# Flamingo-style two-layer block with a top-2 mixture of experts: expert results added to their rows in DRAM instead of on VectorE

## The reference, cut to what matters

```python
def _L1_ffn_ref(x, W_gate, b_gate, W_e, b_e):
    TOP_K = 2
    logits = x @ W_gate + b_gate
    _, top_idx = jax.lax.top_k(logits, TOP_K)
    y_all = jax.nn.relu(jnp.einsum('bsd,edh->bseh', x, W_e) + b_e)
    y = jnp.take_along_axis(y_all, top_idx[..., None], axis=2)
    return y.mean(axis=2)
...
x = x + jnp.tanh(g_ffn[1]) * _L1_ffn_ref(_layernorm(x, axis=-1), ...)
```

## Time and profile before

| | before |
|---|---|
| median of 3 runs | 1082.39 us |
| the profiled execution's own time | 1082.77 us |
| its span (first to last instruction) | 1080.9 us |
| TensorE busy | 959.7 us (89%) |
| VectorE busy | 619.8 us (57%) |
| ScalarE busy | 337.3 us (31%) |
| GpSimd busy | 424.6 us (39%) |
| mean granted TensorE clock | 0.942 of full speed |

### The profile page before, as it was taken

The page is one execution under the profiler, slowest core; times in us unless marked ns, Lnnn a source line. Parts: engine busy times, 40 slices in busy tenths (PEclk is TensorE's granted clock), DMA queues, the critical chain, the costliest instruction groups (busy, mean ns, idle before and its releaser), DMA issues.

```text
span 1080.9 us, 14248 instructions
## 1 busy us (share of the span) xinstructions
PE 959.7 (89%) x4851; PEld 737.6 (68%) x4851; DVE 619.8 (57%) x1067; ACT 337.3 (31%) x599; POOL 424.6 (39%) x414
## 2 busy tenths in 40 slices
PE   4899999999998999999999979979999998629991
PEld 4677778877777777778777658637777674227770
DVE  5864764465752665653647655645655555873334
ACT  4322142132241141331221311225444556312320
POOL 3541522421620522422415243464333424764540
PEclk9899999999999999999999998979999995659996
DMA  8020110010200110200200211060000003213447
GB/s 288 10 79 1 68 40 10 36 43 30 78 1 12 40 39 30 78 1 10 78 1 1 70 44 54 17 226 21 11 10 10 0 1 114 92 56 124 147 127 262
DMA packets 37592, 63.77 MB, mean 59 GB/s; under 512 B 5601, under 2 KB 13217, under 8 KB 37409
## 3 DMA queue, kind: packets, MB, share of 16 engines
q1 hardware_dynamic: 32416, 50.70, 13.7%
q0 software_dynamic: 3680, 12.06, 3.4%
q10 hardware_dynamic: 1440, 0.24, 0.1%
HBM read 52.77 MB, written 10.22 MB: 58 GB/s over the span
## 4 chain that ended last, share of the span: by engine, by line
PE 81%; DVE 8%; issue 4%; DMA 2%; ACT 2%; POOL 2%; ACTq 1%; SPq 0%; POOLq 0%; DVEq 0%
PE ps L1289 17%; PE ps L1290 16%; PE ps L1291 16%; PE ps L1501 5%; PE ps L1378 5%; PE ps L1520 5%; PE ps L1386 4%; PE ps L1508 3%; PE ps L1394 2%; PE ps L1488 2%; DVE at_lo L969 1%; DMA rows_in<-h_rows,gather_i 1%; DVE stats L844 1%; PE ps L1528 1%; POOL k_blk L543 1%
## 5 line engine op out<-in xcount | busy, mean ns | idle before, releaser
L476 POOL TENSOR_TENSOR q_t<-rot_a,rot_b 128x512 f32<-128x512 f32 x64 | 82.3, 1287 | 145.8 <-DVE rot_b L894 145.8
L1289 PE MATMUL ps<-wo_hi,at_hi 128*128 128x512 f32 x256 | 108.7, 425 | 18.7 <-DVE at_lo L969 11.9
L892 DVE TENSOR_TENSOR rot_a<-ps,cos 128x512 f32<-128x512 f32 x80 | 55.3, 692 | 112.6 <-PE ps L1291 112.6
L543 POOL TENSOR_TENSOR k_blk<-k_raw,m_full 32x512 f32<-32x512 f32 x64 | 80.8, 1262 | 90.1 <-ACT k_raw L752 86.3
L1289 PE MATMUL ps<-xt_hi,wq_hi 128*128 128x512 f32 x256 | 108.1, 422 | 0.2 <-issue 0.2
L1291 PE MATMUL ps<-xt_hi,wq_lo 128*128 128x512 f32 x256 | 101.4, 396 | 0.0
L1290 PE MATMUL ps<-xt_lo,wq_hi 128*128 128x512 f32 x256 | 101.4, 396 | 0.0
L1291 PE MATMUL ps<-wo_hi,at_lo 128*128 128x512 f32 x256 | 100.2, 391 | 0.0
L1290 PE MATMUL ps<-wo_lo,at_hi 128*128 128x512 f32 x256 | 100.0, 391 | 0.0
L697 ACT ACTIVATE at_hi<-ps 128x512 fp32r<-128x512 f32 x64 | 38.2, 597 | 189.2 <-PE ps L1394 189.2
L974 DVE TENSOR_TENSOR X<-ps,X 128x512 f32<-128x512 f32 x64 | 44.3, 691 | 84.6 <-PE ps L1291 84.6
(11 more groups left out here) (219 smaller groups left out, 2206.3 us busy)
## 6 DMA issues: line engine op xcount, KB each, us to landing
wq_raw<-in_wq SPq DMA_DIRECT2D x8, 1024.0 KB, 5.6
wo_raw<-in_wo SPq DMA_DIRECT2D x8, 1024.0 KB, 5.3
w_raw<-in_we SPq DMA_DIRECT2D x8, 1024.0 KB, 9.6
y_in<-y_rows SPq DMA_DIRECT2D x16, 256.0 KB, 5.1
X<-in_x SPq DMA_DIRECT2D x4, 512.0 KB, 13.3
wk_raw<-in_wk SPq DMA_DIRECT2D x8, 256.0 KB, 2.8
q_t<-in_ctx_t SPq DMA_DIRECT2D x2, 1024.0 KB, 10.4
wv_raw<-in_wv SPq DMA_DIRECT2D x4, 512.0 KB, 4.5
```

Source lines behind the costliest of these rows:

```text
L476: nc.gpsimd.tensor_tensor(dst, rot_a[:, r % 2, :], rot_b[:, r % 2, :], ALU.add).then_inc(rope_ok, 1)
L543: last = nc.gpsimd.tensor_tensor(k_blk[part, j, grp, :, hd, :], heads(k_raw[part, grp, :]), heads(m_full[part, j, :]), ALU.mult)
L892: nc.vector.tensor_tensor(heads(rot_a[:, r % 2, :]), heads(bank), bcast(cos[:, :], 4), ALU.mult)
L1289: nc.tensor.matmul(dst, w_hi, x_hi, start=start and k == 0, stop=False)
```

## The change

A DRAM tensor `sum_rows` (1024 rows and 128 spare ones) takes the place of `y_rows`. It is filled from `X` before the loop. Each scatter adds its rows to `sum_rows` in the DMA (`compute_op=ALU.add`). Both choices of a row now go to the same DRAM row n, so each scatter waits for the scatter before it to have landed. The factor tanh of the gate is applied by a second ScalarE instruction per tile. The loads into `y_in` and the 16 VectorE additions at the end are gone, and the output is copied from `sum_rows`, DRAM to DRAM. Padding rows of all tiles share the 128 spare rows.

```diff
-        y_rows = nc.dram_tensor("y_rows", (TOP * N + NC * P, D), F32).ap()
+        sum_rows = nc.dram_tensor("sum_rows", (N + P, D), F32).ap()
...
 # SyncE, behind the load of be_b
-            yv = y_rows[0:TOP * N].rearrange("(k b p) d -> p b k d", k=TOP, b=B)
+            for b in range(B):
+                sp.wait_ge(x3_ok, CREDIT + b + 1)
+                sp.dma_start(sum_rows[b * P:(b + 1) * P, :], X[:, b, :]).then_inc(sum_in, 16)
+            sp.dma_start(sum_rows[N:N + P, :], X[:, 0, :]).then_inc(sum_in, 16)
+
             for j in range(3):
                 sp.wait_ge(y_out[j], 16 * ((NT - j + 2) // 3))
-            for q in range(KT):
-                for b in range(2 * q, 2 * q + 2):
-                    for k in range(TOP):
-                        sp.dma_start(y_in[:, b, k, :], yv[:, b, k, :]).then_inc(y_ok[q], 16)
             for b in range(B):
-                sp.wait_ge(x4_ok, CREDIT + b + 1)
-                sp.dma_start(out[b], X[:, b, :]).then_inc(out_done, 16)
+                sp.dma_start(out[b], sum_rows[b * P:(b + 1) * P, :]).then_inc(out_done, 16)
             sp.wait_ge(out_done, 16 * B)
...
 # GpSimd
             def put_rows(i):
                 gp.wait_ge(r_ok, CREDIT + i + 1)
-                nc.gpsimd.indirect_dma_start(y_rows[:, :], bass.IndirectOffsetOnAxis(scatter_i[:, i:i + 1], 0),
-                                             r_d[:, i % 3, :], None).then_inc(y_out[i % 3], 16)
+                if i >= 1:
+                    gp.wait_ge(y_out[(i - 1) % 3], 16 * ((i - 1) // 3) + 16)
+                nc.gpsimd.indirect_dma_start(sum_rows[:, :], bass.IndirectOffsetOnAxis(scatter_i[:, i:i + 1], 0),
+                                             r_d[:, i % 3, :], None, compute_op=ALU.add).then_inc(y_out[i % 3], 16)
...
             gp.wait_ge(si_ok, CREDIT + 1)
+            gp.wait_ge(sum_in, 16 * (B + 1))
             for i in range(NT):
...
 # ScalarE
-                nc.scalar.activation(r_d[:, i % 3, :], ps[:, 4 + i % 4, :], ACT.Relu, scale=1.0 / TOP).then_inc(r_ok, 1)
+                nc.scalar.activation(r_d[:, i % 3, :], ps[:, 4 + i % 4, :], ACT.Relu, scale=1.0 / TOP).then_inc(relu_ok, 1)
+                ac.wait_ge(relu_ok, CREDIT + i + 1)
+                nc.scalar.activation(r_d[:, i % 3, :], r_d[:, i % 3, :], ACT.Copy, scale=tanh_g[:, 3:4]).then_inc(r_ok, 1)
...
 # VectorE
-            nc.vector.tensor_tensor(scatter_i[:, :], padding[:, :], listed[:, :], ALU.add).then_inc(si_ok, 1)
+            nc.vector.tensor_tensor(scatter_i[:, :], padding[:, :], row_of[:, :], ALU.add).then_inc(si_ok, 1)
...
-            for b in range(B):
-                ve.wait_ge(y_ok[b // 2], 64)
-                nc.vector.scalar_tensor_tensor(X[:, b, :], y_in[:, b, 0, :], tanh_g[:, 3:4], X[:, b, :], ALU.mult, ALU.add).then_inc(y0_ok, 1)
-                ve.wait_ge(y0_ok, CREDIT + b + 1)
-                nc.vector.scalar_tensor_tensor(X[:, b, :], y_in[:, b, 1, :], tanh_g[:, 3:4], X[:, b, :], ALU.mult, ALU.add).then_inc(x4_ok, 1)
```

More of the change, by code:

```diff
@@ L190, in flamingo_gated_two_layers @@
         place[0] = at_1
-        y_in = over("y_in", [P, B, TOP, D])
         w_lo = sb("w_lo", [P, EX, KT, D], F32R)
@@ L298, in flamingo_gated_two_layers @@
         of_ok, gi_ok, si_ok = sem("of_ok"), sem("gi_ok"), sem("si_ok")
-        rows_ok, y_out, y_ok = ([sem(f"rows_ok{j}") for j in range(3)], [sem(f"y_out{j}") for j in range(3)],
-                                [sem(f"y_ok{j}") for j in range(KT)])
-        tr_mm, gh_ok, glo_ok, y0_ok = sem("tr_mm"), sem("gh_ok"), sem("glo_ok"), sem("y0_ok")
+        rows_ok, y_out, sum_in, relu_ok = ([sem(f"rows_ok{j}") for j in range(3)], [sem(f"y_out{j}") for j in range(3)], sem("sum_in"),
+                                           sem("relu_ok"))
+        tr_mm, gh_ok, glo_ok = sem("tr_mm"), sem("gh_ok"), sem("glo_ok")
         weh_ok, wel_ok, gate_mm, gt_ok, gt_mm, sel_ok, rank_ok = (sem("weh_ok"), sem("wel_ok"), sem("gate_mm"), sem("gt_ok"), sem("gt_mm"),
                                                            sem("sel_ok"), sem("rank_ok"))
-        y2_mm, td_ok, r_ok, x4_ok, out_done = sem("y2_mm"), sem("td_ok"), sem("r_ok"), sem("x4_ok"), sem("out_done")
+        y2_mm, td_ok, r_ok, out_done = sem("y2_mm"), sem("td_ok"), sem("r_ok"), sem("out_done")
         N_SMALL, N_LATE = 10, 12
@@ L612, in _ @@
             start_counts(ac, (ot_ev, prep_a, gates_ok, hth_ok, cth_ok, wkh_ok, wvh_ok, wqh_ok, wo_hi_ok, v_ok, th_ok, ex_ok, ah_ok, wbh_ok,
-                              lge_ok, zt_ok, pq_ev, p_ok, pt_ok, gelu_ok, weh_ok, r_ok, gt_ok, gh_ok))
+                              lge_ok, zt_ok, pq_ev, p_ok, pt_ok, gelu_ok, weh_ok, relu_ok, r_ok, gt_ok, gh_ok))
             def hi_part(dst, raw, done):
@@ L838, in _ @@
                               x1_ok, bbg_ok, lg_ok, lgm_ok, lgs_ok, lgi_ok, al2_ok, zw_ok, tb_ok, hc_ok, mm_ok, mf_ok,
-                              cv_ok, mx_ok, sb_ok, oi_ok, on_ok, tc_ok, x3_ok, sel_ok, rank_ok, td_ok, x4_ok, wel_v, tri_ok,
-                              slot_ok, hot_ok, of_ok, gi_ok, si_ok, glo_ok, y0_ok))
+                              cv_ok, mx_ok, sb_ok, oi_ok, on_ok, tc_ok, x3_ok, sel_ok, rank_ok, td_ok, wel_v, tri_ok,
+                              slot_ok, hot_ok, of_ok, gi_ok, si_ok, glo_ok))
             def row_stats(n, b, j, ready, before=0):
@@ L1660, in _constants @@
         np.triu(np.ones((P, P)), 1), np.broadcast_to(np.arange(P) - P, (P, P)), np.broadcast_to(P * np.arange(NC + 1), (P, NC + 1)),
-        tok.reshape(P, B * TOP), TOP * N + 1 + np.arange(P)[:, None] + P * np.arange(NC)[None, :],
+        tok.reshape(P, B * TOP), np.broadcast_to(N + 1 + np.arange(P)[:, None], (P, NC)),
         np.broadcast_to(np.arange(NC), (P, NC))], axis=1).astype(np.float32)
```

## The result

The changed kernel takes 1120.04 us (median of 4 runs, 1118.47 to 1121.44) against 1082.32 of the kernel before (one run more than in the median above): a ratio of 1.034, 95% interval 1.0315 to 1.0365, so 3.4% slower. The profiled execution took 1120.19 us with a span of 1118.3. The forecast was 1105 with a range of 1082 to 1145: the right side and inside the range, 15 us too low.

A forecast was written before the change was run, and what follows sets the result against it. The prediction took TensorE and POOL's scatter-gather chain to hold the loop before, and single-file scatters after; 994.9 + 23 L with L = 4.8 gave 1105.3 us (loop +29.9, end -7.4), range 1082 to 1145.

The forecast's parts named there:

- The bound of the loop: Expert loop after the change: scatters run one behind another and set the period, 4.9 us against 3.57 before; chance 68%.
- L: Time of one adding scatter on POOL, from start of issue to landing: taken as 4.8 us, between 3.99 and 5.74.
- The step from landing to the next issue: On POOL between one scatter's landing and the next scatter's issue: taken as 0.1 us, once in each of 22 periods.
- The first scatter: Start of the loop's scatters on POOL: issue at 980.59, which is 979.98 plus 0.61 us for the second ScalarE instruction.
- The end: From the last scatter's issue on: 15.1 us instead of 22.5, a gain of 7.4, with 10 us for the DRAM copies.
- The filling of `sum_rows`: SyncE's 9 stores before the loop: landed by some 958, 22 us before the first scatter waits for them, at no cost.
- The gather's chain of the kernel before: Loop before: gathers queued behind scatters on POOL, 11.0 us per three tiles; the second ScalarE instruction makes it 11.6.
- The wait costs nothing: Rival for the loop: L below 3.77, period 3.87 by the gather's chain, about 1079 us, not slower; chance 15%.
- The dear issue: Rival on POOL: issuing an adding scatter could double or treble the 0.97 us; L = 8 gives 1179 us; chance 9%.
- The clock fell: Rival for TensorE in the loop: low clock level throughout, 6.3 us per tile, 1136 us; chance 8%.

## Why the prediction was right, and where it was short

**The bound of the loop: right.** "the scatters run one behind another, and the whole loop follows them": from the first scatter on the chain after is nothing else, and the run without the wait, with early gathers, takes the period from 5.62 to 3.40.

**L: right in size, and by some luck.** Predicted 4.8, midway between a gather and a gather followed by a plain scatter; the chain shows 4.66 to 5.05 for all but one, and one 5.52, 4.85 on the mean. That the middle of a range from 3.99 to 5.74 came within 0.05 was not worked out from anything. Of the 4.85 us the issue is 1.59, where the prediction had bounds of 0.97 and twice that; the other 3.26 stand against 1.75 of a plain scatter, and no run takes the read and the write in them apart. The rule of the Trainium skill ("Collectives: The Full Stack", why ReduceScatter is half of AllGather) would have given 4.47. The scatter is longer than that; with the issue at its measured 1.59 in place of 0.97 the rule would give 5.09, and the measured 4.85 lies between. The other rule named there ("DMA: Bandwidth & Descriptors", anatomy of one DMA), with its estimate of 3.2 us, is 1.6 us short of the measurement.

**The step from landing to the next issue: wrong, and nearly the whole error.** The prediction wrote: "For that step I take 0.1, as SyncE moved 0.07 after its landing." It was 0.77: 22 x 0.67 = 14.7 us of the 14.9 between 1105.3 and the profiled 1120.2. The small errors of the other terms cancel: L was put 0.05 too low, which makes 1.2 us, the first scatter was put 0.7 too late and the end 0.4 too long. Two things are in the step. The row nearest to the case was not SyncE's but POOL's own, 0.27 from ScalarE's end to the scatter's issue; with it the sum gives 22 x 0.17 = 3.7 us more, 1109, and the kernel with the waits turned round takes 1109.96. The other 0.5 us is the second wait in front of the DMA, which the diff shows and the sum did not price.

**The first scatter** came at 979.93 for 980.59, and so no later than before. The second ScalarE instruction is in it all the same (0.73 us, not 0.61): this execution issued the load `be_b` at 940.34 where the one before did at 941.94, so it was ahead by 1.6 us for reasons outside the change. **The end** took 14.7 us for 15.1, the copies 9.8 for 10. **The filling of `sum_rows`** was hidden, as said: its issues were over at 945.4, and the first scatter still waited for ScalarE.

**The gather's chain of the kernel before: right,** shown twice, by removing it (0.9943) and by lengthening it with the second ScalarE instruction alone (1.0044).

**The rivals.** "The wait costs nothing" needed L below 3.77. With plain scatters, which for the most part are that short, its time came out as worked out: 1079.67 for 1079, period 3.87. The dear issue did not come: 1.59 us. The clock fell to its lower level in parts of the loop, 0.93 and 0.91 on the mean, but not for good, and it set no time in this kernel. It did in the run without the wait.

## What to carry to other kernels

Work that is handed to a DMA as an add is not free when its results meet on the same rows: it turns transfers that nobody waited for into a single file, and each link costs the whole time from issue to landing (here 4.85 us against a period of 3.57). Before such a change compare that time, plus the step to the next issue, with the loop's period. Where a DMA must wait for two semaphores, look in the chain which of them stands as an instruction of its own, and let it be the one that is ready early. And look at what is queued behind a waiting instruction: the best gain of this study in a kernel that computes everything, 0.6%, came from moving a gather ahead of a scatter.

## What was not expected of the hardware

- A wait as an instruction of its own in front of an indirect DMA on POOL costs 0.77 us from the event to the DMA's start, 0.73 of it after the wait has passed; the other wait costs 0.27. That the other one is carried by the DMA itself is inferred from its absence in the chain.
- An adding scatter of 128 rows of 2 KB takes POOL 1.59 us to issue (plain: 0.99) and has more packets. The page's table of queues, first after the change, then for the kernel before:

```profile
q0 software_dynamic: 5152, 12.06, 6.0%
```

```profile
q0 software_dynamic: 3680, 12.06, 3.4%
```

  The same megabytes in 1472 packets more, 64 for each of the 23 scatters, and nearly twice the time on the DMA engines (6.0% for 3.4%, of spans of 1118.3 and 1080.9 us).
- TensorE's clock did not follow how much it had to do. With the waits turned round and early gathers it had about as many matmuls per us as in the changed kernel, and stayed at the full 2.4 GHz in this stretch:

```profile
1010.00:1050.00 40.00, 27.39 (x120) 18.98 (x119) 10.44 (x15) 13.59 (x23) 19.39 (x15) 1.00 0.55 100
```

  That is 120 matmuls in 40 us, 3.0 per us, and 68% busy at a granted clock of 1.00. The changed kernel has 140 in 48 us, 2.9 per us, at 0.93. Its busy share of 74% (35.33 of 48) is no sign of more work, since at the lower level each matmul takes longer (0.43 us for 0.23). What decides between them was not tried.
